# Relation pass of a four-layer graph network: pieces one and two of a bf16 message added by one product of 128 columns, piece three by a product of 64

## The reference

```python
x_src = x[src]
out = jnp.zeros((num_nodes, weight.shape[2]), dtype=x.dtype)
for r in range(num_relations):                # 8
    mask = (edge_type == r)[:, None]
    msg = jnp.where(mask, x_src @ weight[r], 0.0)
    out = out + jax.ops.segment_sum(msg, dst, num_segments=num_nodes)
out = out + x @ self_loop_w.T
return jax.nn.relu(out)
```

## Time and profile before

| what | value |
|---|---|
| median of 3 runs | 4751.88 us (4750.55 to 4753.44) |
| the profiled execution's own time | 4766.78 us |
| its span, first to last instruction | 4765.1 us |
| mean granted clock of TensorE, share of full speed | 0.84 |
| PE busy / weight loads busy | 66% / 52% of the span |
| DVE busy | 68% |
| ACT busy | 30% |
| POOL busy | 31% |
| relation pass, first to last product of `look_up` | 3137.3 to 3830.0 us |

### The profile page before, as it was taken

One profiled execution on the slowest core, in us unless ns is written; L12 is line 12 of the kernel. 1 busy time (PEld: TensorE's weight loads), 2 busy tenths in 40 slices (PEclk: granted clock), 3 DMA queues, 4 the chain that ended last, 5 costly groups with the idle time before them and its releaser, 6 DMA issues. The chain is left out here.

```text
span 4765.1 us, 85791 instructions
## 1 busy us (share of the span) xinstructions
PE 3134.9 (66%) x29646; PEld 2456.5 (52%) x29646; DVE 3234.8 (68%) x7782; ACT 1434.9 (30%) x2734; POOL 1454.1 (31%) x1198
## 2 busy tenths in 40 slices
PE   0155656556550751833849998568888859977995
PEld 0033434333330220211239997348888849977995
DVE  7745545444437979979957775347777759977886
ACT  0023323333320531512539996223333310000000
POOL 0044343444434466446400000046666600000000
PEclk9977777777765985966969998579999969988998
DMA  8733343343343853844837763011111113422331
GB/s 328 296 102 106 112 131 108 107 130 109 104 136 119 262 175 111 263 136 156 262 103 220 222 218 118 24 46 22 22 22 21 22 26 105 110 57 82 90 90 49
DMA packets 413512, 586.45 MB, mean 123 GB/s; under 512 B 79620, under 2 KB 301787, under 8 KB 412709
## 3 DMA queue, kind: packets, MB, share of 16 engines
q1 hardware_dynamic: 366005, 447.16, 31.3%
q0 software_dynamic: 37728, 66.91, 4.8%
q10 hardware_dynamic: 9360, 66.90, 3.5%
HBM read 340.05 MB, written 234.93 MB: 121 GB/s over the span
## 5 line engine op out<-in xcount | busy, mean ns | idle before, releaser
L844 POOL DMA_INDIRECT slots<-bc_rec,idx x496 | 481.1, 970 | 651.8 <-ACT bc_rec L805 502.1
L1253 POOL DMA_INDIRECT rp_rows<-rel_rows,slot_rel x390 | 427.5, 1096 | 425.3 <-POOLq L118 181.9
L1079 PE MATMUL psum<-a_probs,z 128*65 128x512 f32 (+1 forms) x1050 | 448.6, 561 | 142.3 <-DVE a_probs L1020 142.2
L1289 DVE TENSOR_SCALAR rp_hot_src<-rp_key_rows,lane 128x384 bf16<-128x384 f16 x1560 | 381.2, 317 | 212.1 <-ACT rp_key_rows L1414 82.4
L701 DVE TENSOR_SCALAR bc_first_t<-bc_ramp,bc_key_t 128x128 f16<-128x128 f16 x500 | 128.1, 256 | 578.0 <-DMA x<-in_x 421.9
L1501 PE MATMUL psum<-rel_pieces,rp_hot_src 128*128 128x192 bf16 x4680 | 454.4, 249 | 96.1 <-issue 84.2
L483 POOL DMA_INDIRECT slots<-h,idx x192 | 354.3, 1845 | 351.0 <-DMA h<-recs 302.6
L1501 PEld LDWEIGHTS psum<-rel_pieces,rp_hot_src 128*128 128x128 bf16 x4680 | 386.5, 99 | 136.0 <-issue 121.9
L1054 ACT ACTIVATE a_tops<-a_tops,a_s_low 128x1024 f32<-128x1024 f32 (+2 forms) x300 | 284.7, 949 | 568.9 <-DVE a_tops L1011 568.7
L1079 PEld LDWEIGHTS psum<-a_probs,z 128*65 128x65 f32 x1050 | 122.4, 138 | 469.1 <-DVE a_probs L1020 327.5
L1011 DVE SCALAR_TENSOR_TENSOR a_tops<-table,a_s_rest,big 128x1024 f32<-128x1024 f32 (+2 forms) x300 | 313.4, 1045 | 33.1 <-DMA big<-shift_rows 33.1
(11 more groups left out here) (425 smaller groups left out, 6838.5 us busy)
## 6 DMA issues: line engine op xcount, KB each, us to landing
a_counts<-edge_counts SPq DMA_DIRECT2D x150, 512.0 KB
slots<-big ACTq DMA_DIRECT2D x65, 1005.0 KB
ep_rec<-slots SPq DMA_DIRECT2D x65, 1005.0 KB, 7.3
edge_counts<-bc_counts SPq DMA_DIRECT2D x12, 3125.0 KB
hot_rows<-ep_hot_src SPq DMA_DIRECT2D x325, 96.0 KB, 4.5
sp_hot_src<-hot_rows SPq DMA_DIRECT2D x325, 96.0 KB, 2.0
sq_hot_src<-hot_rows SPq DMA_DIRECT2D x325, 96.0 KB, 1.9
a_counts<-edge_counts SPq DMA_DIRECT2D x75, 282.5 KB
```

What stands on the lines that cost most here:

```text
L844: pool.indirect_dma_start(k.slots, bass.IndirectOffsetOnAxis(k.idx[:, first + t:first + t + 1], 0), rec[:, j, t, :], None).then_inc(scatte ...
L1079: last = nc.tensor.matmul(sums[:, a:b], k.z[:, s, 0:D + 1], probs[:, a:b], start=s == 0, stop=True, skip_group_check=True)
L1253: pool.indirect_dma_start(rows[:, n % ROW_SLOTS, s, 0:width], None, table, bass.IndirectOffsetOnAxis(k.slot_rel[:, at:at + 1], 0))\
L1289: last = v.tensor_scalar(hot_src[:, n % HOT_SLOTS, rel, :], key_rows[:, n % 2, :], k.lane[:, rel:rel + 1], None, ALU.is_equal)
```

## The change

In the relation pass the triple's bank, `totals` and the placed rows are 128 columns wide for each bin instead of 64 (384 instead of 192 columns a bank). For a looked-up slot, one product of 128 columns adds piece 1 to columns 0 to 64 and piece 2 to columns 64 to 128; a second one adds piece 3 to columns 0 to 64. A gathered slot adds to columns 0 to 64 as before. When all is placed, DVE adds columns 64 to 128 of `k.acc` to columns 0 to 64, once, ahead of the loop over the left tiles.

```diff
-        wide = cols
+        wide = 2 * D if relations else cols
         totals = sb("totals", [BIN_ROWS, 2, SLOTS, wide])
...
                 for y in range(2):
                     dve.wait_ge(placed[y], parts_placed(y, NTRIPLE))
+                if relations:
+                    chain.link(v.tensor_tensor(k.acc[:, :, 0:D], k.acc[:, :, 0:D], k.acc[:, :, D:2 * D], ALU.add))
                 left_count = dve.value_load(k.left_tiles[0:1, 0:1], min_val=1, max_val=EPAD // P)
...
                         if relations and looks_up(c):
-                            for piece in range(3):
-                                got = msg[:, LOOKUP_NO[c] % MSG_SLOTS, s, piece * D:(piece + 1) * D]
-                                last = nc.tensor.matmul(to, hot_dst16[:, y, s, :], got, start=first and piece == 0, stop=True,
-                                                        skip_group_check=True)
+                            got = msg[:, LOOKUP_NO[c] % MSG_SLOTS, s, :]
+                            nc.tensor.matmul(to, hot_dst16[:, y, s, :], got[:, 0:2 * D], start=first, stop=True,
+                                             skip_group_check=True)
+                            last = nc.tensor.matmul(to[:, 0:D], hot_dst16[:, y, s, :], got[:, 2 * D:3 * D], start=False,
+                                                    stop=True, skip_group_check=True)
                         else:
                             got = rows[:, n % ROW_SLOTS, s, :] if relations else msg[:, c % MSG_SLOTS, s, :]
-                            last = nc.tensor.matmul(to, hot_dst[:, y, s, :], got, start=first, stop=True,
+                            last = nc.tensor.matmul(to[:, 0:D] if relations else to, hot_dst[:, y, s, :], got, start=first, stop=True,
                                                     skip_group_check=True)
```

## The result

The changed kernel takes 4723.77 us (median of 4 runs, 4723.07 to 4725.69), the kernel before 4751.22 us (4 runs of the same session, 4748.00 to 4753.44): ratio 0.9939, interval 0.9916 to 0.9963. It is faster by 27.5 us. The prediction had 4740.3 us and a range down to 4730: the direction was right, the size and the range were wrong. Two later sessions gave 0.9883 and 0.9914 for the same kernel. (A session is one batch of measurements on one chip, always with the kernel before beside the others; the recorded expectations say "call".) The profiled execution's own time is 4724.03 us.

The account below looks back on a forecast made before the run. PE was taken as the fullest engine, losing time to something that goes with the gathers. Products -13.5, evacuation +0.16 and +1.0, final addition +0.7 gave -11.6 us: 4751.9 to 4740.3 us, range 4730 to 4751.

Parts of the forecast that it names:

- The product's price: Relation pass, PE: a looked-up block falls from 0.355 us to 286 ns, -13.5 us for 195 blocks, ends -9 and +10.
- The second rival: Looked-up blocks: the 84-wide load isn't hidden behind 128 columns, block 406 ns, +10.0 us and +1.9 fixed, 4763.8 us; chance 0.08.
- Evacuation: Copies of the wider bank take 487 ns in place of 328: +0.16 us for the last, +1.0 for the other twelve.
- Placing and the final addition: End of the pass: wider placed rows cost nothing, DVE's one addition of 1.83 us lies partly on the path, +0.7 us.
- The first rival: Late completions make each group's third look-up wait; only one block in three counts, -2.6 us, 4749.3 us; chance 0.22.
- the chain theory: While POOL gathers, each group's third look-up waits for the keys' completion, ACT, then DVE; earlier keys give 9.3 us or less.
- the prediction's two readings of the late ACT: ACT starts at 3506.67, keys' products recorded at 3504.35: PE runs later than recorded, or its completions are reported late.
- The step that failed: Groups while POOL gathers: some 1.8 us lost a group, going by gathers, whose number stays at 390, so nothing saved there.
- The third rival: Groups while gathering: loss goes per instruction PE takes in, 18 of 240 fewer save 7.5%, 8.8 us, 4731.5 us; chance 0.14.
- The argument against that rival: The near pass takes in more instructions per us, 18 and 12 in 0.98 us, and loses nothing, so loss goes by gathers.
- PE's clock: Short spells at 1.2 instead of 2.4 GHz, which a less busy PE could see more of; only widens the range, no chance.

Follow-up runs that it names:

- after_nogather: The changed kernel with the relation pass's gathers left out, POOL zeroing the gathered rows once: 4585.81 us, ratio 0.9606 to the kernel before.
- early_keys_again: The changed kernel with keys spelled on PE and taken by ACT two chunks earlier, in a session with the loss: 4714.59 us, 0.9917 to the kernel before.
- only_middle: The changed kernel with the new form only in the block behind a group's second look-up, nine products in the other two: 4185.53 us, one run.
- only_outer: The changed kernel with the new form only in the two blocks behind a group's third look-up, nine products in the other: 4178.40 us, one run.
- after_third_time: The changed kernel, unchanged, traced in one session with the kernel before: 4718.61 us, ratio 0.9914.
- before_again: The kernel before, unchanged, traced in one session with the changed kernel: 4756.39 us, one run.
- small_third: The changed kernel with one more pair a slot, of 32-wide weights and one column that nobody reads: 4767.80 us, 1.0015 to the kernel before.
- early_keys: The changed kernel with keys spelled on PE and taken by ACT two chunks earlier, in the session without the loss: 4165.96 us, 0.9965 to the kernel before.
- six_wide: The changed kernel with piece 3 also added by a product of 128 columns, the last 64 zeros: 4721.01 us, 0.9903 to the kernel before.
- after: The changed kernel itself in the first session: 4723.77 us, ratio 0.9939 to the kernel before.
- nine_apart: The changed kernel's wide bank with nine products of 64 columns kept, pieces 1 and 2 by products of their own: 4785.63 us, 1.0005 to the kernel before.
- spell_quarter: The changed kernel with each product that spells keys cut in four of 32 columns: 4856.27 us, 1.0207 to the kernel before.
- after_again: The changed kernel, unchanged, run again on the chip that had been free of the loss: 4726.16 us, 0.9883 to the kernel before.

## Why the prediction was right and wrong

- **The product's price: right.** The block 0.27 us (0.286), the free group 8.16 us (8.17), the pass without gathers 13.2 us shorter (13.5). The second rival, the unhidden load, fell with the first timeline.
- **Evacuation: the last one right, the others cost nothing.** 487 ns, as forecast. I had put +1.0 us on the other twelve; in after_nogather every group from 5 to 57 takes 8.16 or 8.17 us, those with an evacuation too (a test without gathers alone).
- **Placing and the final addition: right.** +0.75 us in the profile, 0.86 forecast.
- **The first rival fell by its size.** It left 4.5 us for the products, and the pass became 33 us shorter. The chain of the earlier trace rows doesn't set the pace: the gaps ahead of look-ups stayed with the change (31.7 and 35.5 us), and early_keys_again, which took nearly all of them away, still needed 9.77 us a group, where the chain theory expected 9.3 or less. only_middle and only_outer, meant to test this rival, ran in the session without a loss and couldn't. Of the prediction's two readings of the late ACT neither was settled: where ACT stood waiting for a look-up, its cast started 0.04 us behind the modelled end of the last product without gathers, and 1.36 us behind it in after_third_time (0.49 in before_again, medians).
- **The step that failed** is the one that took the time lost while gathering (1.8 us a group) as fixed, with "the loss goes by gathers, whose number stays at 390" as the reason. The loss does need the gathers, and their number did stay, but the conclusion doesn't follow: how much is lost also goes by what PE has to take in. The third rival had this, with 0.14 and 8.8 us. Its direction held and its size was too small: it made the loss proportional to the number (7.5% less), and the loss fell from 149 to 126 us in session E, by 15%, and from 148 to 128 in the first session: 20 us that the sum had put at nothing. If PE takes in an instruction every 43 ns and the work runs beside that, as small_third suggests, 18 fewer save 0.77 us a group; 0.60 were measured, 0.22 of them the products' own price.
- **A sign was in the trace already.** The earlier trace rows shows 17 products behind the gap of 1.16 us, but a look-up has 24; the other seven stand behind a second gap, which no wait can explain:

```profile
3511.19 0.74 PE L1501 MATMUL psum<-rel_pieces,rp_hot_src 128*128 128x192 bf16 x7 [0.30 <-issue]
```

  Such gaps inside look-ups sum to 41 us in groups 5 to 57 of that trace, those ahead of look-ups to 27.
- **The argument against that rival** was the near pass, which takes in more instructions per us and loses nothing. That pass has no gathers, so it told nothing on what one instruction costs while they run.
- **PE's clock** was no case of its own. Behind the first group of the pass, the granted clock stood at 1.2 GHz for 37.5 us in before_again and for 27.3 us in after_third_time, and never in the two kernels without gathers. At half speed a low spell costs at most half its length, so the clock can hold 5 of the 36 us.
- **The difference in sizes.** The change gains 27 us in one session, 40 and 61 in others. The loss itself differs between sessions, from nothing (B) to 142 us in the changed kernel's pass (C, 673.1 - 531.4). The changed kernel didn't run in session B; early_keys, which holds the change, gained 17 us there (0.9965, interval 0.9945 to 0.9986), and the pair without gathers lies 10 us apart.

No version beat the changed kernel clearly: early_keys has 0.9917 in D and six_wide 0.9903 in A, beside the change's 0.9914 in E and 0.9883 in C, but neither ran beside it in one session.

## What to carry to other kernels

Price a product from back-to-back rows where nothing disturbs them, then look whether the stage runs at that price; where it doesn't, find out what the excess counts (instructions, columns, waits) before treating it as a constant. A gap inside a run of products that no wait divides is not a dependency. In a stage where POOL issues indirect DMAs densely, judge an edit by how many pairs of load and product it takes from PE as much as by its busy time, and compare only within one session.

## What the runs showed of the hardware

- While POOL issued some 30 indirect DMAs in 50 us, a group of PE's work of 8.2 to 8.6 us took 1.6 to 2.9 us longer (after 1.70, nine_apart 2.68, spell_quarter 2.88); small_third, with 10.26 us of work, took 0.57 longer. At 13 DMAs in 50 us nothing was lost, at 24 a part; in session B nothing at 38. The same kernel took 4182.97 and 4787.26 us on one chip in two sessions. Nearly all of that lies where indirect DMAs and PE's work meet: between the traces early_keys (B) and after_again (C), 417 us in the sorting stage and 142 us in this pass, of 559 us between the spans.
- An 84-wide load of bf16 weights is hidden behind a product of 128 columns: such a pair with one of 64 columns takes 0.09 us, and a pair takes 55 ns where all products have 128 columns (six_wide, six in 0.33 us).
- A pair of 32-wide weights and one column between 84-wide pairs brings the slot from 0.09 to 0.31 us, with 0.11 to 0.16 us between starts (small_third). Whether the change of width, the single column or its place in PSUM costs this wasn't taken apart.
